# Cross-attention with a feed-forward chain: attention in rounds of two key chunks

## What is computed

```python
def attention(q, k, v):                       # 16 heads of 32
    scores = jnp.einsum('bqhd,bkhd->bhqk', q, k) * scale
    probs = jax.nn.softmax(scores, axis=-1)
    return jnp.einsum('bhqk,bkhd->bqhd', probs, v)
...
q = rms_norm(linear(x, q_w, q_b), norm_q_w).reshape(B, L, NH, HD)
...
img_x = attention(q, k_img, v_img)            # keys 0 to 256
txt_x = attention(q, k, v)                    # keys 257 to 1023
out = (txt_x + img_x).reshape(B, L, DIM)
return linear(out, o_w, o_b)
...
x_norm = layer_norm(x, in_gamma, in_beta)
thought = x_norm[:, -1, :] @ agg_w + agg_b
for _ in range(K_STEPS):                      # 4
    t = layer_norm(thought, pn_gamma, pn_beta)
    t = jax.nn.gelu(t @ d1_w + d1_b, approximate=False)
    thought = thought + (t @ d2_w + d2_b)
broadcast = (thought @ bc_w + bc_b)[:, None, :]
gate = jax.nn.sigmoid(x @ gate_w + gate_b)
return layer_norm(x + gate * broadcast, out_gamma, out_beta)
```

## Time and profile before

| | us |
|---|---|
| median of 3 runs | 610.68 (607.62 to 612.35) |
| profiled execution, first to last instruction | 607.0 |
| PE busy | 533.4 (88%) |
| DVE busy | 392.7 (65%) |
| ACT busy | 282.7 (47%) |
| POOL busy | 240.7 (40%) |
| granted TensorE clock, mean | 0.941 |

### The profile page before, as it was taken

The page is one execution under the profiler, slowest core; times in us unless marked ns, Lnnn a source line. Parts: engine busy times, 40 slices in busy tenths (PEclk is TensorE's granted clock), DMA queues, the critical chain, the costliest instruction groups (busy, mean ns, idle before and its releaser), DMA issues.

```text
span 607.0 us, 9796 instructions
## 1 busy us (share of the span) xinstructions
PE 533.4 (88%) x3768; PEld 325.9 (54%) x3768; DVE 392.7 (65%) x750; ACT 282.7 (47%) x504; POOL 240.7 (40%) x138
## 2 busy tenths in 40 slices
PE   2589799999978999989999988898998998999860
PEld 2478668987644555545555454454444544554320
DVE  5547886433965787558776686476565747368676
ACT  3355744552124566426565253536362443376342
POOL 0032330032024766545655533243333345467453
PEclk9988989999979999979999998899999998799976
DMA  7506667599469699927888571707061713100001
GB/s 284 169 1 242 238 248 278 171 209 313 157 165 317 146 214 239 223 88 171 204 214 214 159 170 71 170 10 163 26 146 71 170 37 109 71 1 35 17 37 52
DMA packets 56327, 91.35 MB, mean 150 GB/s; under 512 B 5316, under 2 KB 30276, under 8 KB 55768
## 3 DMA queue, kind: packets, MB, share of 16 engines
q1 hardware_dynamic: 52032, 74.93, 45.8%
q0 software_dynamic: 3184, 14.16, 7.2%
q10 hardware_dynamic: 1064, 1.63, 1.0%
HBM read 70.84 MB, written 19.40 MB: 149 GB/s over the span
## 4 chain that ended last, share of the span: by engine, by line
PE 70%; DVE 16%; ACT 5%; POOL 3%; issue 2%; DMA 2%; SPq 0%; POOLq 0%; ACTq 0%; DVEq 0%
PE psum L673 14%; PE psum L767 12%; PE psum L730 10%; PE psum L748 10%; PE psum L772 5%; PE psum L802 5%; DVE negt L1154 4%; PE psum L891 3%; PE psum L856 3%; PE psum L837 2%; DMA qst<-crow 1%; DVE negm L1152 1%; DVE attT L1170 1%; POOL ssum L1323 1%; POOL ssum L1321 1%
## 5 line engine op out<-in xcount | busy, mean ns | idle before, releaser
L999 ACT ACTIVATE prob<-psum 128x512 f32<-128x512 f32 x256 | 138.6, 593 | 179.9 <-PE psum L748 175.0
L1154 DVE TENSOR_REDUCE negt<-psum 128x1 f32<-128x255 f32 (+1 forms) x256 | 129.2, 545 | 0.0
L1371 POOL TENSOR_TENSOR added<-added,prob 128x1024 f32<-128x1024 f32 x48 | 114.0, 2375 | 24.4 <-ACT prob L999 19.9
L730 PE MATMUL psum<-kst,qst 96*128 96x512 f32 x256 | 100.3, 468 | 5.3 <-DVE negt L1154 5.2
L1368 POOL TENSOR_TENSOR added<-prob 128x1024 f32<-128x1024 f32 x16 | 39.5, 2466 | 158.7 <-ACT prob L999 158.7
L1152 DVE TENSOR_REDUCE negm<-psum 128x1 f32<-128x257 f32 x128 | 53.6, 418 | 74.2 <-PE psum L730 73.6
L748 PE MATMUL psum<-qst,kst 100*128 100x256 f32 x512 | 94.9, 306 | 4.7 <-DMA qst<-crow 3.4
L767 PE MATMUL psum<-prob,vring 128*32 128x256 f32 x1152 | 94.1, 411 | 1.7 <-issue 0.5
L748 PEld LDWEIGHTS psum<-qst,kst 100*128 100x128 f32 x512 | 81.8, 200 | 24.5 <-ACT prob L999 9.6
L730 PEld LDWEIGHTS psum<-kst,qst 96*128 96x128 f32 x256 | 41.4, 195 | 67.5 <-issue 39.6
L1321 POOL TENSOR_TENSOR ssum<-sq 128x512 f32<-128x512 f32 x6 | 9.5, 1585 | 110.7 <-ACT sq L964 110.7
(11 more groups left out here) (150 smaller groups left out, 664.4 us busy)
## 6 DMA issues: line engine op xcount, KB each, us to landing
kst<-kscr SPq DMA_DIRECT2D x96, 256.0 KB, 5.4
vring<-vscr SPq DMA_DIRECT2D x16, 576.0 KB, 8.5
kscr<-hl SPq DMA_DIRECT2D x16, 512.0 KB, 3.0
d<-d POOLq DMA_DIRECT2D x8, 1024.0 KB, 8.3
qst<-qscr SPq DMA_DIRECT2D x96, 64.0 KB, 5.9
vscr<-vbuf SPq DMA_DIRECT2D x18, 256.0 KB, 3.2
raw<-ctxT SPq DMA_DIRECT2D x4, 1024.0 KB, 5.2
qscr<-hl SPq DMA_DIRECT2D x8, 512.0 KB, 3.7
```

The costliest lines, as they stand in the source:

```text
L730: pe.matmul(psum[:, n % 3, :], qst[0:96, slot, jj, qt * P:(qt + 1) * P], kst[0:96, slot, jj, half * 512:(half + 1) * 512], start=True, sto ...
L999: act.activation(prob[:, r % NP, part], score2[:, part], ACT.Exp).then_inc(exp2_done, 1)
L1154: dve.tensor_reduce(negt[:, u % 2, qt, half, j:j + 1], psum[:, n % 3, k0:512], AX.X, ALU.max, negate=True)\
L1371: pool.tensor_tensor(added[:, :], added[:, :], prob[:, r % NP, :], ALU.add).then_inc(added_done, 1)
```

## The change

Attention is worked in blocks of two rounds r and r + 1 (r even). A block issues on PE: S2 of r (both halves), S1 of t (both halves), then a half of S2 of r + 1, a half of S1 of t + 1, and again one of each; then the steps that stood in round r; then PV of r - 2 and r - 1; then the steps that stood in round r + 1. PV comes up to two rounds later than its scores. S1 and S2 are split into steps of one half each.

The eviction of a unit (attn) is three steps, each behind a half of S2 in the block with r % 8 == 2, and weigh stands at the end of that block's scores. Shift stands in the middle of the scores of the block with r % 8 == 4, maxes ahead of them. The output projections move from rounds 2 and 3 of a unit to 4 and 5, and the chain starts two steps later (s = 8 * 8 + 7). The image half's sum of chunk 5 is issued in its own PV and no longer in the next one's. Numbers of instructions are the same.

```diff
@@ -172,11 +177,11 @@
-    s = 8 * 8 + 5
+    s = 8 * 8 + 7
...
-        s = 8 * NG * (k + 1) + 2
+        s = 8 * NG * (k + 1) + (4 if k < 3 else 2)
...
     for t in range(10, ahead):
-        add('S1', t)
-    last = max(max(extra), 8 * NU + 1)
-    for r in range(last + 1):
-        if r < 8 * NU:
-            add('S2', r)
-            if r % 8 == 0 and r > 0 and r // 8 + 2 < NU:
-                add('load', r // 8 + 2)
-            if r % 8 == 1 and r // 8 + 1 < NU and r > 8:
-                add('load_v', r // 8 + 1)
-        if 1 <= r <= 8 * NU:
-            add('PV', r - 1)
-            if r % 8 == 0:
-                add('attn', r // 8 - 1)
-        if r % 8 == 1 and 8 < r <= 8 * NU + 1:
-            add('weigh', r // 8 - 1)
-        t = r + ahead
-        if t % 8 == 0 and t // 8 <= NU:
-            add('maxes', t // 8 - 1)
+        s1(t)
+    last = max(max(extra), 8 * NU + 2)
+
+    def side(r):
         if r == 2:
             add('late', r)
         elif r % 8 == 7 and r // 8 < XS:
             add('bias', r // 8)
         elif r % 8 == 5 and r < 64:
             add('late', 3 + r // 8)
-        for e in extra.get(r, []):
-            plan.append(e)
-        if t < 8 * NU:
-            add('S1', t)
-        if t % 8 == 0 and t <= 8 * NU:
+
+    def extras(r):
+        plan.extend(extra.get(r, []))
+        plan.extend(post.get(r, []))
+
+    for r in range(0, last + 1, 2):
+        t = r + ahead
+        u = r // 8 - 1
+        scores, keys, evict = r < 8 * NU, t < 8 * NU, r % 8 == 2 and 0 <= u < NU - 1
+        if t % 8 == 0 and t // 8 <= NU:
+            add('maxes', t // 8 - 1)
+        if scores:
+            add('S2', r, 0)
+            add('S2', r, 1)
+            if r % 8 == 0 and r > 0 and r // 8 + 2 < NU:
+                add('load', r // 8 + 2)
+        if evict:
+            add('attn', u, 0)
+        if keys:
+            s1(t)
+        if t % 8 == 0 and t // 8 <= NU:
             add('shift', t // 8 - 1)
-        plan += post.get(r, [])
+        if scores:
+            add('S2', r + 1, 0)
+        if evict:
+            add('attn', u, 1)
+        if keys:
+            add('S1', t + 1, 0)
+        if scores:
+            add('S2', r + 1, 1)
+        if evict:
+            add('attn', u, 2)
+        if keys:
+            add('S1', t + 1, 1)
+        if evict:
+            add('weigh', u)
+        side(r)
+        extras(r)
+        if 2 <= r <= 8 * NU:
+            add('PV', r - 2)
+            add('PV', r - 1)
+            if r == 8 * NU:
+                for part in range(3):
+                    add('attn', NU - 1, part)
+                add('weigh', NU - 1)
+        if r % 8 == 0 and 8 <= r and r // 8 + 1 < NU:
+            add('load_v', r // 8 + 1)
+        side(r + 1)
+        extras(r + 1)
     return plan
...
+            def S2(r, half):
                 u, c = r // 8, r % 8
...
                 k0 = ORDER[c] * P
-                for j in range(HPG):
+                if r > 0:
+                    pe.wait_ge(exp2_done, 2 * r - 1 + half)
+                for j in (2 * half, 2 * half + 1):
                     slot, jj, _ = pair_slot(u, j)
-                    if r > 0 and j % 2 == 0:
-                        pe.wait_ge(exp2_done, 2 * r - 1 + j // 2)
                     mm = pe.matmul(score2[:, j * QH:(j + 1) * QH], kst[0:100, slot, jj, k0:k0 + P],
                                    qst[0:100, slot, jj, :], start=True, stop=True)
-                    if j % 2 == 1:
-                        mm.then_inc(s2_done, 1)
...
-                                       source[:, j * QH:(j + 1) * QH], start=first, stop=last)
+                                       source[:, j * QH:(j + 1) * QH], start=first, stop=last, skip_group_check=True)
                     return mm
 
                 if c == N_ADDED:
-                    mm = add_sum(2, prob[:, r % NP, :], 1, True, False)
+                    add_sum(2, prob[:, r % NP, :], 1, True, False)
+                    mm = add_sum(1, prob[:, r % NP, :], 0, False, False)
                 elif c == N_ADDED + 1:
                     pe.wait_ge(added_done, (N_ADDED - 1) * (u + 1))
                     add_sum(0, added, 1, False, True)
-                    add_sum(1, prob[:, (r - 1) % NP, :], 0, True, False)
                     mm = add_sum(0, prob[:, r % NP, :], 0, False, False)
                 elif c == N_ADDED + 2:
                     mm = add_sum(0, prob[:, r % NP, :], 0, False, True)
@@ -986,28 +1017,29 @@
             def vimg(b):
...
-                if r >= NP:
+            def S2(r, half):
+                if r >= NP and half == 0:
                     u, c = (r - NP) // 8, (r - NP) % 8
 
-                    act.wait_ge(pv_done, r - NP + 1 + (c == N_ADDED))
+                    act.wait_ge(pv_done, r - NP + 1)
                     if c < N_ADDED:
                         act.wait_ge(added_done, (N_ADDED - 1) * u + max(c, 1))
-                for n in range(2):
-                    part = slice(512 * n, 512 * (n + 1))
-                    act.wait_ge(s2_done, 2 * r + n + 1)
-                    act.activation(prob[:, r % NP, part], score2[:, part], ACT.Exp).then_inc(exp2_done, 1)
-
-            def attn(u):
-                act.wait_ge(pv_done, 8 * (u + 1))
-                if u >= 1:
-                    act.wait_ge(attn_done, u)
-                act.copy(pvc[:].rearrange("p s n -> p (s n)"), psum[:, PV_BANK, :]).then_inc(pv_emptied, 1)
+                part = slice(512 * half, 512 * (half + 1))
+                act.wait_ge(s2_done, 2 * r + half + 1)
+                act.activation(prob[:, r % NP, part], score2[:, part], ACT.Exp).then_inc(exp2_done, 1)
+
+            def attn(u, part):
                 r = rsum[:].rearrange("p s n -> p (s n)")
-
-                act.activation(r, psum[:, SUM_BANK, :], ACT.Ln).then_inc(pv_emptied, 1)
-                act.wait_ge(pv_emptied, 2 * (u + 1))
-                act.activation(r, r, ACT.Exp, scale=-1.0).then_inc(rsum_done, 1)
+                if part == 0:
+                    act.wait_ge(pv_done, 8 * (u + 1))
+                    if u >= 1:
+                        act.wait_ge(attn_done, u)
+                    act.copy(pvc[:].rearrange("p s n -> p (s n)"), psum[:, PV_BANK, :]).then_inc(pv_emptied, 1)
+                elif part == 1:
+                    act.activation(r, psum[:, SUM_BANK, :], ACT.Ln).then_inc(pv_emptied, 1)
+                else:
+                    act.wait_ge(pv_emptied, 2 * (u + 1))
+                    act.activation(r, r, ACT.Exp, scale=-1.0).then_inc(rsum_done, 1)
```

More of the change, by code:

```diff
@@ L77, in proj, with s1 @@
                 add('proj', tile, oc, piece)
+    def s1(t):
+        add('S1', t, 0)
+        add('S1', t, 1)
     def v(b, chunks):
@@ L166, in make_plan @@
     extra, post = {}, {}
+    shifts = range(4, 8 * NU, 8)
     def at(step, *e):
@@ L173, in closed @@
     def closed(s):
-        while any((s + n + ahead) % 8 == 1 for n in range(1, KC // CHUNKS)):
+        while any(s + n in shifts for n in range(1, KC // CHUNKS)):
             s += 1
         return s
-    s = 8 * 8 + 5
+    s = 8 * 8 + 7
     at(s, 'ch_row')
@@ L215, in make_plan @@
             s = max(s, 8 * NU + 2)
-        while (s + 4 + ahead) % 8 == 1 and s + 4 < 8 * NU:
+        while s + 4 in shifts:
             s += 1
@@ L299, in build @@
     in_plan = {e: n for n, e in enumerate(plan)}
-    n_late = next(n for n, e in enumerate(jobs) if in_plan[e] > in_plan[('S1', 8 * NU - 1)] and e[0].startswith('f_'))
+    n_late = next(n for n, e in enumerate(jobs) if in_plan[e] > in_plan[('S1', 8 * NU - 1, 1)] and e[0].startswith('f_'))
     for n in range(n_late, len(jobs)):
```

52 lines of the change are left out of this document (24 added, 28 removed).

## The result

The changed kernel takes **702.92 us** (median, 701.8 to 703.31) against 609.15 (605.6 to 612.35): ratio 1.1546, 95% interval 1.1493 to 1.1598. That is 94 us slower, where I had forecast 43 more (654 us), and it lies outside my range of 611 to 676. Its profiled span is 699.8 us, 92.8 more than before; the mean granted clock is 0.876 instead of 0.941.

The account below looks back on a forecast made before the run. TensorE sets the pace. 27 - 1.2 - 1 + 4 + 3 + 4.1 + 2.5 + 5 = +43.4 on the span of 607.0, plus 3.7 around it: 654 us; 8 in 10 from 611 to 676.

Parts of the forecast that it names:

- Plain block: Blocks of two rounds with S1: waiting for ACT replaces most of the saved crossing, 3.36 against 3.41 us, 0.05 saved.
- rival (b): Crossing saved in full, the wait for ACT hidden and the chain no worse: 589, some 592 with the end; chance 0.1.
- Eviction: Block evicting a unit: PV waits 0.87 us for the emptied banks, and the block ends at 4.23.
- The weighing, the maxima and the shift: Nine units: neighbouring DVE operations meet POOL's adds and delay the transpose, +2.97 us per unit, +27 in all.
- rival (c): Minimum blocked too, or clock at 1.2 GHz behind every shift: 22 us more, 676; chance 0.1.
- TensorE's clock: Waits of 3 us in nine places can bring the 1.2 GHz level: 0 to 31 us, taken as +5.
- The output projections: Moved away from the shift, waits in units 4 and 8 go, DVE's work on o is late: -1.2 us.
- The chain: Five units from r 76: -1 for 20 blocks, +4 for the steps, +3 for the weighing meeting adds.
- The last six blocks: Blocks from r 116, with no S1 left to cover the exponential: 6 x 0.68, +4.1 us.
- The end: After the last PV: 20 chain steps left instead of 19, and the last eviction loses its cover, +2.5 us.
- Rival (a): No blocking on DVE by POOL's adds: around 625 us, 611 with the chain at its low bound; chance 0.2.
- the middle case: The forecast itself for the whole kernel, 654 us with its own spread 632 to 672; chance 0.6.

Follow-up runs that it names:

- small adds: POOL's adds cut from 1024 to 32 columns, most of the sum left out: changed kernel 621.56 us, kernel before 598.52 us.
- the run with POOL waiting: Changed kernel with one wait added, POOL's second add of a unit also waiting for the minimum: 628.65 us.
- The copy early: Changed kernel with POOL's adds cut to 32 columns and ACT's copy ahead of the eviction block's first exponential: 606.44 us.
- The last run: Changed kernel with POOL's second add waiting for the minimum, ACT's copy ahead of the exponentials, and eight gate products moved behind the last value products: 617.65 us.

## Why the prediction was off, point by point

- **Plain block, 3.36 instead of 3.41.** Right in its mechanism: S2 waits for ACT at 1.27 (1.25). PV begins at 2.43 of the block, not 2.36, and 4.73 less three further sets of 0.43 leaves 3.44, so nothing is saved, where I had 0.05. Units without adds in the way take 17.33, +0.2 on 17.12 and +0.4 on the 16.94 of the kernel before with small adds; I had 0.3. That answers rival (b) as well: 6.7 us of PE time are saved in units 1 to 8, the span is not shorter.
- **Eviction, 4.23 with PV waiting 0.87.** Right: 4.25 and 0.78.
- **The weighing, the maxima and the shift, +2.97 per unit, +27.** The mechanism was the right one and carried the sign; the size was not. The step that failed is "the minimum ends at 8.4": I gave it 0.2 us behind the second weighing, although by my own schedule the fourth add was ready and POOL worked without a pause to 10. The trace shows the minimum held until that fourth add ends: it is 2.92 long even where only a load stands between the adds, 3.93 to 4.15 where the bias addition follows too. So the transpose waited 5.7 to 6.9 us in units 1 to 7, not 3.3; unit 8, where no fourth add was ready, is what I had forecast, with 2.93. In units 1 to 8 these waits sum to 48.3 us, where mine make 26. I had written a whole add of 2.4 for the minimum down as the bound (+5.4 per unit; 3.3 + 2.4 is the 5.7 of units 6 and 7) and as rival (c), with a chance of 0.1; the row of the second weighing was already the pattern for each further operation of this kind. POOL's weight load and bias addition I left out although they are in POOL's list in just these rounds; moving the load alone returned 16 us.
- **TensorE's clock, +5.** Too small. Each long wait was followed by a stretch at 1.2 GHz: behind the transpose of 351.04 4.07 us instead of 2.26, that is 1.8 in this unit. The same difference in each of units 1 to 8 is 1.4 to 1.9 us, 13 together. The units 1 to 8 ran at a mean of 0.84 against 0.99 in the run with POOL waiting. Forecast for units 1 to 9 with o and clock was 31; units 1 to 8 alone took 61.2.
- **The output projections, -1.2.** Not to be seen in the changed kernel. With POOL waiting, units 4 and 8 took 26.06 and 25.95 against 29.40 and 25.45: -2.8 together, the 2.8 that I took off. But that is luck: unit 4 gained 3.3, its wait of 1.57 and the fall of its clock (0.88 before, 1.00 there), and unit 8, where I had 1.2 off, lost 0.5.
- **The chain, -1, +4 and +3 in units 9 to 13.** +9.0 in all, 2 to 3 of it what I had booked for unit 9 in the 27. But the split was off: with POOL waiting these units are 2.5 us shorter than before, and with small adds in both kernels 0.7 longer. So my +4 for the steps, less 1 for the blocks, was too much, and the hold on DVE costs 11.5 there, not 3.
- **The last six blocks, +4.1.** Mis-sized: +11.1 in units 14 and 15, +7.2 with POOL waiting and +11.7 with small adds in both kernels. So the length of the adds doesn't explain it. In the changed kernel ACT waits 4.4 us for added buffers there, behind POOL's channel multiplications, and PE 6.9 for exponentials. The copy early takes 3.7 us off with small adds. How the rest divides between the waits for ACT and POOL's queue I have not separated.
- **The end, +2.5.** +10.7, and +9.1 with POOL waiting. Of it 6.0 lie between the last score product and the last o (13.5 against 7.5 us), 1.7 in the projection (8.82 against 7.12, at the lower clock), 3.0 behind. Of the 6.0, 3.4 are value products and sums (6.3 against 2.9 us) that in blocks only stand behind the last score product, and so come out of units 14 and 15; 2.1 are the lost cover of the eviction (a wait of 2.57 against 0.45), which I had named. The last run took that wait away, and its median can't tell what came back. The rest is argued from the traces, no run took it away.
- **Ahead of unit 1** I booked nothing. It is 0.8 us in the changed kernel and 2.9 with POOL waiting. Unit 0 takes 23.9 us in both, against 21.2 before: unit 1's first scores wait 6.37 and 6.74 us for the DMA of their shift row, against 1.81. The row is sent earlier than before, at 183.96 instead of 187.37, but its DMA takes 10.7 us to land instead of 6.8; why is open. What lies ahead of attention took 171.5 us in the profiled execution of the changed kernel and 173.5 and 173.7 in the other two, which hides part of it.

Rival (a), no hold on DVE, would have been 625; the run with POOL waiting is this case made true, and took 628.65. That they are so near is in part luck: the chain cost 2.5 us less than before, not 6 more, and the last units and the end 16 more, not 7.

The chosen 0.6 for the middle case was the mistake of judgement: with three operations in a row and adds back to back, that each waits for a whole add was the plain reading of the earlier trace rows, and 5.4 per unit, plus a clock fall of 1.8 us behind each as measured afterwards, would have given about 687 with the rest as it was.

## What to carry over

Before VectorE operations with two SBUF operands are moved, list what POOL has *ready* during the whole time they would take, its DMA issues and odd additions too, and count at least one whole POOL operation for each of them: small operands didn't make it cheaper here. When PE waits for the last of such operations, try letting POOL wait: one semaphore on the second add returned 74 of 94 us with no instruction moved. And a saving on PE that merges chunks should be priced together with everything that the merging makes neighbours, in the steady units and in the last ones.

## What the runs showed of the hardware

- A minimum of 128x8 elements took 0.15 to 0.17 us alone, 1.5 beside an add that was in progress, 2.30 when it had to come between two adds that follow each other, 2.92 with a weight load issued by POOL between them and up to 4.15 with a 128x512 addition as well.
- For a VectorE instruction with two SBUF inputs beside a GpSimd one, "SBUF — State Buffer" of the Trainium skill (Who interferes with whom) says that who issues first decides. For the weighings of unit 6 the trace agrees: the third add had begun at 345.17, the second weighing at 345.61. For the minimum it doesn't: its record begins at 347.98 and the fourth add's only at 348.51, behind POOL's DMA issue, and yet the minimum ends 0.04 behind that add. Why is open.
- The hold works in the other direction too: the add that began while the first weighing ran took 2.60 us instead of 2.38 (two in 5.12 us, 0.1 between them, against 4.90 for two in the run with POOL waiting).
- DVE reductions from PSUM beside the same adds kept their 0.40 to 0.42 and 0.68 us.
- By the starts of one round, a pair of crossings between 32-column products and full-array ones came to 0.33 to 0.34 us. Halving their number took 0.78 us off PE's busy time in a plain unit (16.21 with POOL waiting against 16.99), 0.2 for each of four pairs, less than the starts say; the ends of matmuls are modelled.
